# Feed-forward stack on one core: the output projection moved ahead of the last quarter of the products

## The reference, cut to what matters

```python
for i in range(6):
    x = attn_layer(shift_tokens(x), Wqkv[i], q_scale[i], k_scale[i], Wo[i]) + x
    x = ffn_layer(shift_tokens(x), ln_g[i], ln_b[i], W1[i], b1[i], W2[i], b2[i]) + x
```

## Time and profile before

| what | value |
|---|---|
| median of 3 runs | 4923.8 us (4920.8 to 4928.75) |
| the profiled execution | 4914.5 us, span of its instructions 4912.7 us |
| TensorE matmul busy | 4174.3 us (85%) |
| VectorE / GpSimd / ScalarE busy | 3474.2 / 2722.8 / 2303.1 us |
| mean granted TensorE clock | 0.921 |

### The profile page before, as it was taken

The page is one execution under the profiler, slowest core; times in us unless marked ns, Lnnn a source line. Parts: engine busy times, 40 slices in busy tenths (PEclk is TensorE's granted clock), DMA queues, the critical chain, the costliest instruction groups (busy, mean ns, idle before and its releaser), DMA issues. The chain is left out here.

```text
span 4912.7 us, 195171 instructions
## 1 busy us (share of the span) xinstructions
PE 4174.3 (85%) x89432; PEld 2525.8 (51%) x89432; DVE 3474.2 (71%) x4350; ACT 2303.1 (47%) x3018; POOL 2722.8 (55%) x2228
## 2 busy tenths in 40 slices
PE   5555469999999999999967776799999999999997
PEld 2111136666666666656632222566666666566664
DVE  7999957777777777777744342677777777777774
ACT  4554524455455455454413333345545455455543
POOL 5776646666666666666500000666666666666662
PEclk6777679999999999999969998899999999999998
DMA  0000011212112121111100001121121211212110
GB/s 17 1 1 1 1 48 31 64 33 60 33 33 60 33 61 32 45 48 33 29 6 1 1 1 35 30 60 33 33 60 33 60 33 33 60 33 62 32 33 24
DMA packets 85116, 162.85 MB, mean 33 GB/s; under 512 B 33228, under 2 KB 54472, under 8 KB 81224
## 3 DMA queue, kind: packets, MB, share of 16 engines
q1 hardware_dynamic: 84296, 150.36, 10.7%
HBM read 48.61 MB, written 1.05 MB: 10 GB/s over the span
## 5 line engine op out<-in xcount | busy, mean ns | idle before, releaser
L1059 PEld LDWEIGHTS banks<-f_P_T,f_V_previous 32*64 32x64 f32 x24576 | 486.3, 132 | 538.7 <-issue 528.2
L1293 POOL TENSOR_TENSOR f_q_rotated<-f_rope_aq,f_rope_bq 128x1024 f32<-128x1024 f32 x192 | 455.8, 2374 | 401.9 <-DVE f_rope_bq L1348 401.1
L1059 PE MATMUL banks<-f_P_T,f_V 32*64 32x32 f32 x24576 | 575.7, 224 | 53.9 <-issue 53.2
L1059 PE MATMUL banks<-f_P_T,f_V_previous 32*64 32x32 f32 x24576 | 566.4, 228 | 57.4 <-issue 50.3
L1029 PE MATMUL banks<-f_wqkv,H 128*128 128x512 f32 x1152 | 573.7, 622 | 46.8 <-DMA f_wqkv<-in_L_ffn_Wqkv 20.0
L1345 DVE TENSOR_TENSOR f_rope_aq<-banks,f_rope 128x1024 f32<-128x1024 f32 x192 | 235.1, 1225 | 489.3 <-ACT f_sqq L1208 443.9
L1293 POOL TENSOR_TENSOR f_k_rotated<-f_rope_ak,f_rope_bk 128x1024 f32<-128x1024 f32 x192 | 451.6, 2352 | 220.3 <-DVE f_rope_bk L1348 220.3
L1029 PE MATMUL banks<-f_wqkv,G 128*128 128x512 f32 x1152 | 554.9, 604 | 0.0
L493 POOL TENSOR_TENSOR poly_F<-poly_F 128x1024 f32<-128x1024 f32 (+1 forms) x192 | 400.7, 2114 | 181.4 <-ACT poly_F L477 181.3
L1059 PEld LDWEIGHTS banks<-f_P_T,f_V 32*64 32x64 f32 x24576 | 450.7, 134 | 61.2 <-issue 59.3
L1208 ACT ACTIVATE f_sqq<-banks 128x1024 f32<-128x1024 f32 x192 | 197.2, 1027 | 525.9 <-PE banks L1029 525.9
(11 more groups left out here) (173 smaller groups left out, 8572.0 us busy)
## 6 DMA issues: line engine op xcount, KB each, us to landing
f_V_previous<-f_V SPq DMA_DIRECT2D x192, 384.0 KB, 3.6
f_V_previous<-f_V SPq DMA_DIRECT2D x192, 128.0 KB, 2.3
f_wqkv<-in_L_ffn_Wqkv SPq DMA_DIRECT2D x12, 1536.0 KB, 7.9
f_rope<-in_rope SPq DMA_DIRECT2D x12, 1024.0 KB, 8.7
f_wo<-in_L_ffn_Wo SPq DMA_DIRECT2D x12, 512.0 KB, 10.7
f_w<-in_L_ffn_W SPq DMA_DIRECT2D x12, 341.0 KB
f_w<-in_L_ffn_W SPq DMA_DIRECT2D x24, 64.0 KB
xin<-in_L_attn_a_x SPq DMA_DIRECT2D x2, 512.0 KB, 4.9
```

The lines of the kernel that those rows point to most:

```text
L1059: mm = nc.tensor.matmul(banks[i * DH:(i + 1) * DH, g * BLK + k * W:g * BLK + (k + 1) * W], of[n % 3][r, h * DH:(h + 1) * DH], PT[n % 2][r, ...
L1293: nc.gpsimd.tensor_tensor(qk[i][:], ra[i][:], rb[i][:], ALU.add).then_inc(radd.sem, 1)
```

## The change

The wait on `sbd` leaves `feed_third` and stands in the slot's body behind part three of the products. The output projection of tile n-3 comes directly behind that wait, then part four, then the pieces of `feed_third` and `feed_fourth`. No other engine's program is changed.

```diff
--- before.py
+++ after.py
@@ -1104,10 +1104,6 @@
 
             def feed_third(s):
 
-                if live(s - 1):
-                    pe.wait_ge(sbd.sem, sbd.at(tile(s) - 1))
-                else:
-                    bank5_free(s - 1)
                 if (b := feed(s, 9)) is not None:
                     hidden(b, 1, 2, 5, f_g.sem)
                 if (b := feed(s, 12)) is not None:
@@ -1184,10 +1180,10 @@
                 feed_second(s)
                 if live(s - 2):
                     values(n - 2, 4, 6)
-                feed_third(s)
-                if live(s - 2):
-                    values(n - 2, 6, 8)
-                feed_fourth(s)
+                if live(s - 1):
+                    pe.wait_ge(sbd.sem, sbd.at(n - 1))
+                else:
+                    bank5_free(s - 1)
                 if live(s - 3):
 
                     if (s - 3) % LAYER == 0:
@@ -1199,6 +1195,10 @@
                         mm = nc.tensor.matmul(bank(4, P), wo[layer(s - 3) % 2][:, k, :], OT[(n - 3) % 2][:, :, k, :],
                                               start=k == 0, stop=k == HP - 1)
                     mm.then_inc(y_mm.sem, 1)
+                if live(s - 2):
+                    values(n - 2, 6, 8)
+                feed_third(s)
+                feed_fourth(s)
 
         @block.scalar
         def _(act):
```

## The result

Over four executions the changed kernel takes 5008.0 us (5005.6 to 5019.3) against 4926.3 us (4920.8 to 4931.2) before: ratio 1.0171, 95% interval 1.0151 to 1.0190. It is 1.7% slower. The profiled execution took 5006.8 us, its span 5005.0 us, 92.3 us more than before.

The account below looks back on a forecast made before the run. TensorE, 95% busy, bounds the kernel. Uncovered copy, late add and 2 us of tail cost 103 us; returned stalls give 41 and 11, clock 0: +51 us on 4923.8, rounded to 4975 us, range 4932 to 5035.

Parts of the forecast that it names:

- term 1: Before the next slot's Q projection: with y moved, TensorE waits for ScalarE's now uncovered copy of O_T; 72 us.
- term 2: After slots with s mod 4 = 0: VectorE's adds of y end late, delaying the next Q transposes 0.70 us; 29 us.
- term 3: Behind part three: y gives the instruction supply time, so TensorE's issue stalls go; 41 us back, 11 more in early slots.
- term 4: Granted clock falling after TensorE stalls: most old falls go (-19 us), new idle brings 11 falls (+19); net 0 us.
- nothing comes back: Rival: the issue stalls have another cause or merely move to the next block edge; 5037 us, chance 0.18.
- Supply was the real bound: Rival: with y between the parts all issue stalls go, those of weight loads included; faster, 4879 us, chance 0.08.

## Why the prediction was right, and where its sizes were off

The forecast was slower, +51 us, and it was slower, by 84. The range held it. Step by step:

- *y is the cover of the copy* (term 1): right. Kind 2 slots wait 1.11 us, as the third slot of a call had shown, and a shorter copy shortens the wait. Behind kinds 1 and 3 Q waits about as computed, behind kind 0 it does not.
- *The add is late behind kind 0* (term 2): right, 0.83 us a slot instead of 0.70. VectorE to TensorE took 0.14 us, not 0.06.
- *The sizes of terms 1 and 2* were too small: 103 us, where the slots give about 150. Over 22 slots of each kind in both calls it is 44 x 1.56 (kind 2), 44 x 1.19 (kind 1) and 44 x 0.67 (kind 3), 151 us; the first nine slots of the calls add 12 (they took 2 us more although 10 of stalls went), and the k transposes take off 12. Two prices were missing. A run of products that is parted costs some 0.27 us (kinds 2 and 3, about 25 us). And a matmul group that starts after a real wait holds TensorE 0.10 us longer: Q to the transposes takes 1.82 us at 1629.96, 1.72 in the earlier trace rows; over 130 such starts 13 us. With both, kind 3 is 0.26 + 0.27 + 0.10 = 0.63, for 0.67 measured.
- *The late stalls come back* (term 3): right, to the microsecond by luck: 38.9 to 1.8 us plus overlaps is 40, for 41; the early slots gave 9 or 10 of 11. That the stalls are the instruction supply was argued in the forecast and is shown now. One number of that argument was wrong by two: the two parts that run together hold 128 matmul records with a weight load each, 256 instructions in 1.4 us, not 512 in 1.6. The term came from counted stalls and does not change with it. The Trainium skill, Runtime: NRT & Kernel Launch, section Instruction fetch mechanics, has the block of 256 instructions, which the places modulo 256 bear out; its "mostly hidden" does not hold for this kernel, where TensorE lost 42.5 us to it in the slots of the weight loads and 52 in the other steady slots (9 to 94).
- *The clock breaks even* (term 4): wrong. The falls behind late stalls went, 51 us at low clock to 7, but the 11 new ones did not come. That returned 22 us (half of 44) where I had 0. A lone idle of 1.1 us with a dense Q projection behind it brought the clock down in one of 44 slots at most. This miss hid about half of the missing cost: +47 on the cost, -22 on the clock. Some 8 us more came back as stalls too small to be listed (0.12 us a slot in kind 3 and 0.06 in kind 2, on average over slots without a listed one).
- *Not in the forecast*: the slots of the weight loads took 6 us more than their share of the kind 1 term (20.0 for 12 x 1.19), kind 0 slots 6.6 us (more stalls ahead of part four among them), and 12 us lie outside the slots, most of it scatter. With +17 net of the misses above and +3 of stalls that did not return (49 of 52) that is some 45 us, for the 41 by which the profiled execution missed the forecast (92 for 51). The sum closes to the scatter of the unchanged parts, not better. By the medians the miss is 33 us.

That the total came out only 33 us off is thus in part luck: a cost 47 us too low stood against 30 us of clock and small stalls that the forecast did not count on.

Of the rivals, "nothing comes back" (5037) lay about as near to the result as my forecast (4975), but as a mechanism it is wrong: the stalls did go. "Supply was the real bound" was wrong for this change and half right about the kernel. The stalls at the weight loads, which I had left alone as beyond reach of y, were indeed untouched by it (42.5 to 46.0 us), yet worth 58 us to an edit that goes at them.

Open: the rows show where the 0.27 us of a parted run lie, but not why two parts run faster together than apart; and why the clock did not fall behind the new waits was not tested.

## What to carry to other kernels

Before moving work to an earlier place, ask what it covered where it stood. Here the last block of a slot was the cover of an eviction and of an add on two other engines. Half of it in its old place covered most of the eviction, and half of it between the products took away four fifths of the late stalls (38.9 to 7.3 us). A bound engine's idle time with no releaser is worth counting by instruction number: if it falls on block ends, spread out dense runs of small instructions with long ones, and keep large transfers out of their way.

## What the runs showed of the hardware that I had not expected

- Packets of the instruction queue (16.4 KB; stalls come every 256 instructions or a multiple of it) started no closer than 3.2 us apart, and a TensorE that had stalled for 0.5 us or more went on 2.2 to 3.0 us after such a packet had started. Two parts of the products use up 256 instructions in 1.4 us.
- Behind 3.6 MB of weights issued at once TensorE stalled for 3.3 to 6.3 us; with pieces of about 512 KB the longest stall in the two steady stretches was 2.6 us.
- One long matmul of four instructions (1 us) behind part three took away 33 us of stalls and 48 us at low clock, and so paid for about half of what its own executions cost (an estimate of 103 us, 1.2 us each less the k transposes' 12; 51 measured).
